# A macaron block on one core: W2 sums in four column groups, the b2 rows by a broadcast load, and the slot table ahead of the expert list

## The chip, the cores and the metric

One of the cores of a Trainium2 chip runs the kernel. The metric is the device time of one execution in microseconds (us); three executions of the kernel before were timed, and their median stands for it.

## The reference, cut to what matters

The input x has 8 batches of 256 tokens of 128 numbers. The whole is a macaron: x + 0.5 FFN(norm x), then x + attention(norm x), then x + 0.5 FFN(norm x), with the same FFN weights in both halves. The FFN is a mixture of 8 experts, of which each token takes the 2 with the largest router logits:

```
logits = xt @ Wr + br;  probs, idx = top_k(softmax(logits), 2)
h = layernorm(relu(xt @ W1[e] + b1[e])) * g1[e] + be1[e]      # 512 wide
y = layernorm(relu(h @ W2[e] + b2[e])) * g2[e] + be2[e]       # 128 wide
out = sum over the token's two experts of gate * y
```

The kernel folds the inner layernorm's g1 and be1 into W2 and b2. The product of a normalized row with g1*W2 needs W2's rows scaled by g1, less their mean over the 512 rows (the sum of g1*W2 over the rows, divided by 512), and b2 needs the sum of be1*W2 added. These sums over the rows of W2, for g1 and for be1 and for each of 8 experts, are the "W2 sums" of this change.

## The kernel before, in words

Each engine runs its own program, in an order written out by hand, and waits on semaphores. The span has a front (routing of all tokens for the first FFN, and preparing the weights), then 39 tiles of 128 sorted token slots in pairs through the experts (first FFN), then attention, then the second FFN. Only the front changes.

The front in the order of the engines:

- SyncE issues the loads: x, Wr, the rows g1, be1, b1 (into `rows`, 96 partitions), b1 again, b2 (one row, into partition 16 of `wmix`), be2, W1 (2 MB), W2 (2 MB), the attention weights, and later the store of the normalized rows.
- GpSimd clears `wmix` (L2410), builds `ones` and the identity, issues the broadcast loads of br and g2, builds the two selection matrices `sel17` and `mask16` and the other constants, splits b1 (`bias_parts`), waits until all 16 tiles are normalized, builds tables and `mask_factors`, adds the last count to `s_ld_a` (L2480), and then gathers the rows of the tiles with indirect transfers (L513), two tiles for each pair.
- TensorE runs 30 products of `ones` (L2495) once the identity is there, then in turns the transposes of the normalized rows (L943) and the logits (L950), the centred W1 of experts 0 to 2 (`hidden_weights`, L2351 and L2352), the ranks, W1 of experts 3 to 5, the first W2 sums (L2378), the 32 slot products (L1037), W1 of experts 6 and 7, the second W2 sums, the transposed gates (L1046), and the first pairs with the "own products" (L1111, L1112) between them.
- The W2 sums are four accumulating products for each half of the experts. Each has 16 columns of `cols` as its stationary operand (g1 and be1 of 8 experts for one chunk of 128 rows) and 4 experts of W2 (512 columns) as its moving one, and they add up in one bank, rows 0 to 15. ScalarE then masks the rows (`own_rows`, L715) into `wmix`. TensorE's own products spread them: with `sel17[0]` to the mean over all partitions (bank 3 or 4), with `sel17[1]` to the be1 sums plus the b2 row of partition 16 (bank 6 or 7).
- VectorE does the layernorm statistics (L1187) and rows (L1196), the choice of the experts, ranks and slot positions, and the one-hot operands of the slot products (L1342 to L1346). After them come the sorted experts (L1348 to L1357), the lambda of attention (L1359, L1360), the slot table (L1362 to L1365), the packed expert numbers (L1216 to L1220), the gates (L1269 to L1276), and the two halves of `center_weights` (L2369), which subtract the spread mean from the scaled W2.
- ScalarE copies between PSUM and SBUF, scales W2 by g1 (L802, 32 tiles of 128x128), then does the exponentials of gates and lambda (L809, L811), `own_rows(0)`, W1 of experts 6 and 7 back, the first copy of turned rows (L747), `own_rows(1)`, and the two copies into `b2p` (L876).

The first pair's transposes of the hidden rows (`turn_h`) wait for the first copy into `b2p`; `hidden(1, ...)` waits for both halves of the centring, and `second(0, ...)` for the second copy.

Of the kernel before, what the change touches and what calls it, by code (L numbers as in the profile page):

```python
# [17 lines left out]
ALU = mybir.AluOpType  # L18
ACT = mybir.ActivationFunctionType
X = mybir.AxisListType.X  # L20
# [88 lines left out]
def build(nc, x, Wq, Wk, Wv, Wo, lq1, lk1, lq2, lk2, Wr, br, W1, b1, g1, be1, W2, b2, g2, be2, out, stages=("f1", "at", "f2")):  # L109
    with ExitStack() as ctx:  # L110
# [26 lines left out]
        cols = sb("cols", [P, 96])  # L137
# [3 lines left out]
        mask16 = sb("mask16", [16, NE])  # L141
# [183 lines left out]
        past8 = ordering[0:1, 1344:1344 + 48]  # L325

# [19 lines left out]
        N_IDENT, N_REP, N_EPS, N_MASK, N_CENTER, N_ROWS, NCONST, N_ORDER = 1, 2, 3, 5, 6, 12, 16, 17  # L346
        NMASK, NBIAS = 18, 10
# [432 lines left out]
        def moe_scalar(act, S, first):  # L780
# [3 lines left out]
            if first:  # L784
                deviations(act, S, 0, 4)
                for g in range(1, 4):
                    deviations(act, S, g, 4)
                    turned_rows(act, S, g - 1, first)
                    if g == 1:
                        act.wait_ge(s_cols, 1)  # L790
                        act.copy(cols[:], bank[6][:, 0:96]).then_inc(s_colc, 1)
# [15 lines left out]
                scaled(1)  # L807
                act.wait_ge(S["top"], 1)
# [5 lines left out]
                own_rows(act, 0)  # L814
# [182 lines left out]
        def moe_tensor(pe, S, first):  # L997
# [3 lines left out]

            if first:
                turn_rows(pe, S, 0, first)
                pe.wait_ge(s_ld_w, 16 * 7)
# [28 lines left out]
                weight_sums(pe, 0, range(FC))  # L1033
# [75 lines left out]
            def own_products(h):  # L1109
                pe.wait_ge(s_mixed, h + 1)  # L1110
                pe.matmul(bank[3 + h][:], sel17[:, 0, :], wmix[:, 512 * h:512 * h + 512], start=True, stop=True).then_inc(s_wmix, 1)  # L1111
                pe.matmul(bank[6 + h][:], sel17[:, 1, :], wmix[:, 512 * h:512 * h + 512], start=True, stop=True).then_inc(s_b2m, 1)  # L1112

            if first:
                pe.wait_ge(s_colc, 2 + NE - 1)
                turn_x(0, 0, 0)
                own_products(0)
# [3 lines left out]
                own_products(1)  # L1121
# [4 lines left out]
                turn_x(2, 1, 0)  # L1126
                pe.wait_ge(s_w2c, 2)
                hidden(1, 1, e[2:4])
# [158 lines left out]
        def first_routing(dve, S, step):  # L1287
# [59 lines left out]

            step.begin(dve.tensor_tensor(ends16[0:1, 0:NE], offsets[0:1, 0:NE], rows16[0:1, 0:NE], ALU.add))  # L1348
# [9 lines left out]
            dve.wait_ge(s_ld_a, 80)  # L1358
            step(dve.tensor_tensor(lam_p[:], lam_in[:, 0:4:2, :], lam_in[:, 1:4:2, :], ALU.mult))  # L1359
            dve.tensor_reduce(lam_s[:], lam_p[:], X, ALU.add).then_inc(A["lam"], 1)  # L1360
            dve.wait_ge(S["slotp"], 1)
            step(dve.tensor_copy(slot_t[:], bank[5][:, 0:40]))  # L1362
            step(dve.scalar_tensor_tensor(slot_f[:], bank[5][:, 40:80], float(YBASE), slot_t[:], ALU.mult, ALU.add))
            step(dve.tensor_scalar(slot_i[:], slot_f[:], float(TOPK * TOK - YBASE), None, ALU.add))
            dve.tensor_scalar(slot_u[:], slot_i[:], TOPK * TOK - 1, 1, ALU.bitwise_and, ALU.logical_shift_right).then_inc(S["slot"], 1)  # L1365
# [965 lines left out]
        def bias_parts(pool, st):  # L2331
            pool.wait_ge(s_dve, 1)
            pool.wait_ge(s_ld_w, 16 * 7)
# [26 lines left out]

        def center_weights(dve, step):
            dve.wait_ge(s_bc, 16)
            w2cv = w2c[:].rearrange("p (a c d) -> p a c d", a=NE, c=FC)
            for h in range(2):
# [6 lines left out]
                last.then_inc(s_w2c, 1)  # L2371

# [159 lines left out]
```

## Time and profile before

| | us |
|---|---|
| three executions | 447.38, 447.42, 450.34 |
| median | 447.42 |
| profiled execution: span from first to last instruction | 444.6 |
| TensorE busy in the span | 395.1 |
| VectorE busy in the span | 348.4 |

The profiled execution has no time of its own on the page; its span is 2.8 us under the median, and these 2.8 us lie before the first and behind the last instruction. The span is cut into 40 slices on the page; TensorE is at 70% or more in all of them, and its granted clock is full but for two stretches, one in the front and one early in attention. In the views that follow times count from the span's start.

### The profile page before, as it was taken

The numbers are of one execution on the slowest core, as the hardware profiler recorded it, in microseconds if no ns is written. First come the engines' busy times: TensorE is split into PE (matmuls) and PEld (weight loads), VectorE is DVE, ScalarE is ACT, GpSimd is POOL, SyncE is SP. The second block draws the span as 40 slices with busy tenths as digits, with TensorE's granted clock in tenths as the row PEclk, the third lists the DMA queues.
The fourth block names the chain that finished last, engine by engine and source line by source line (L and its number), as shares of the span: only waits on it lengthen the run. The fifth ranks groups of instructions, "written<-read, shape, count | busy, mean of one in ns | idle before, by whom it ended". The sixth has DMA issues, their size and how long they took to land.

```text
span 444.6 us, 11683 instructions
## 1 busy us (share of the span) xinstructions
PE 395.1 (89%) x3605; PEld 278.5 (63%) x3606; DVE 348.4 (78%) x1302; ACT 286.7 (64%) x589; POOL 246.8 (56%) x348
## 2 busy tenths in 40 slices
PE   7989999999898857889888889976899899999984
PEld 7735487877676744556564656554577677878733
DVE  5886578887959886878897988976688968788865
ACT  1395687755676754787677777764765467667630
POOL 8685554436461136374847566576634758555540
PEclk9996999999999955999999999999999899999999
DMA  7920114554443411000000001001121221111127
GB/s 219 335 96 14 35 49 143 181 178 158 121 144 112 170 37 35 21 8 20 25 13 25 24 21 33 25 27 36 56 60 34 72 64 56 53 59 47 37 72 244
DMA packets 25862, 35.17 MB, mean 79 GB/s; under 512 B 4282, under 2 KB 18546, under 8 KB 24659
## 3 DMA queue, kind: packets, MB, share of 16 engines
q1 hardware_dynamic: 20866, 24.62, 16.7%
q0 software_dynamic: 4944, 9.90, 7.6%
q8 instruction: 28, 0.46, 0.4%
q14 instruction: 24, 0.19, 0.1%
HBM read 15.45 MB, written 18.24 MB: 76 GB/s over the span
## 4 chain that ended last, share of the span: by engine, by line
PE 51%; DVE 20%; issue 9%; POOL 8%; ACT 5%; DMA 3%; DVEq 1%; SPq 1%; POOLq 0%; ACTq 0%
PE bank L972 11%; PE bank L991 10%; PE bank L981 5%; DVE mx L2134 4%; POOL xr_scratch L459 3%; PE bank L1181 3%; PE bank L2495 2%; PE bank L1900 2%; DMA early<-y_scratch 2%; PE bank L1176 2%; ACT early L1712 1%; PE bank L1918 1%; POOL orr L1658 1%; PE bank L1852 1%; DMA y_scratch<-yo,dest_u 1%
## 5 line engine op out<-in xcount | busy, mean ns | idle before, releaser
L991 PEld LDWEIGHTS bank<-w2c,hT 128*128 128x128 f32 x624 | 76.5, 194 | 23.5 <-issue 22.6
L991 PE MATMUL bank<-w2c,hT 128*128 x624 | 78.1, 279 | 4.9 <-ACT hT L760 4.9
L972 PE MATMUL bank<-w1s,xT 128*128 x156 | 74.1, 596 | 0.7 <-DVE w2c L2369 0.6
L2134 DVE TENSOR_REDUCE mx<-bank 128x4 f32<-128x1024 f32 (+1 forms) x48 | 58.5, 1220 | 13.7 <-PE bank L1861 13.3
L1712 ACT ACTIVATE early<-bank 128x768 f32<-128x768 f32 x64 | 51.8, 812 | 23.7 <-PE bank L1908 23.0
L1377 DVE BATCH_NORM_STATS2 st<-wide 128x6 f32<-128x512 f32 x78 | 50.1, 683 | 19.8 <-ACT wide L754 19.7
L760 ACT COPY hT<-bank 128x1024 f32<-128x1024 f32 (+1 forms) x40 | 39.5, 988 | 34.0 <-PE bank L981 34.0
L513 POOL DMA_INDIRECT xgw<-xn_scratch,slot_u x39 | 37.4, 960 | 35.4 <-PE bank L961 24.3
L483 POOL DMA_INDIRECT y_scratch<-yo,dest_u x39 | 39.0, 1001 | 31.3 <-PE bank L981 16.8
L579 POOL DMA_INDIRECT yk<-y_scratch,posi x32 | 32.2, 1005 | 42.2 <-DMA y_scratch<-yo 17.4
L754 ACT ACTIVATE wide<-bank 128x1024 f32<-128x1024 f32 (+1 forms) x40 | 40.0, 1001 | 10.3 <-PE bank L972 9.6
L459 POOL DMA_INDIRECT xr_scratch<-row_buf,hi_i x32 | 31.8, 994 | 22.6 <-PE bank L1908 12.9
L981 PE MATMUL bank<-ident,wide 128*128 128x128 f32 x312 | 40.9, 274 | 1.3 <-issue 1.3
L972 PEld LDWEIGHTS bank<-w1s,xT 128*128 128x128 f32 x156 | 27.0, 190 | 22.0 <-issue 21.6
L981 PEld LDWEIGHTS bank<-ident,wide 128*128 128x128 f32 x312 | 35.3, 142 | 2.6 <-issue 2.0
L937 ACT COPY wide<-bank 128x1024 bf16<-128x1024 bf16 x28 | 28.4, 1014 | 5.7 <-PE bank L1181 5.6
L775 ACT ACTIVATE yo<-yz,r 128x128 f32<-128x128 f32 x78 | 27.1, 396 | 4.2 <-DVE yz L1420 2.6
L1396 DVE SCALAR_TENSOR_TENSOR yy<-bank,r,b2p 128x128 f32<-128x128 f32 x78 | 24.6, 351 | 6.1 <-DVE r L1390 1.6
L1900 PE MATMUL bank<-mxT,sel 64*128 64x384 bf16 x128 | 22.2, 343 | 7.2 <-ACT early L1712 5.1
L1852 PE MATMUL bank<-mrhs,mlhs 64*128 64x128 bf16 (+1 forms) x192 | 16.1, 248 | 11.4 <-DVE mx L2134 6.6
L1420 DVE SCALAR_TENSOR_TENSOR yz<-yy,mv,g2b 128x128 f32<-128x128 f32 x78 | 23.3, 339 | 0.0
L559 POOL TENSOR_TENSOR ars<-ave,neg_half 128x2 f32<-128x2 f32 x8 | 5.8, 720 | 31.2 <-DVE ave L2092 31.2
(380 smaller groups left out, 893.4 us busy)
## 6 DMA issues: line engine op xcount, KB each, us to landing
xr_scratch<-row_buf SPq DMA_DIRECT2D x8, 1032.0 KB
xgw<-xr_scratch SPq DMA_DIRECT2D x39, 64.5 KB, 1.8
y_scratch<-yo SPq DMA_DIRECT2D x19, 128.0 KB, 1.8
w1s<-in_L_ffn_W_dram SPq DMA_DIRECT2D x1, 2048.0 KB, 9.9
early<-y_scratch SPq DMA_DIRECT2D x8, 256.0 KB, 3.4
xn_scratch<-row_buf SPq DMA_DIRECT2D x1, 1024.0 KB
out_dram<-xs SPq DMA_DIRECT2D x8, 128.0 KB, 2.6
row_buf<-row_buf SPq DMA_DIRECT2D x6, 128.0 KB
```

Of the source, the lines that this page charges most:

```text
L459: pool.indirect_dma_start(out=xr_dram, out_offset=bass.IndirectOffsetOnAxis(ap=slot2[:, c:c + 1], axis=0), in_=rows_of[t // HALF][:, t % H ...
L483: pool.indirect_dma_start(out=y_dram, out_offset=bass.IndirectOffsetOnAxis(ap=dest_u[:, 2 * p + j:2 * p + j + 1], axis=0), in_=yo[:, p % 2 ...
L513: pool.indirect_dma_start(out=xg[:, u, :], out_offset=None, in_=xn_dram, in_offset=bass.IndirectOffsetOnAxis(ap=slot_u[:, n:n + 1], axis=0 ...
L579: pool.indirect_dma_start(out=yk4[:, t % (2 * YRING), k, :], out_offset=None, in_=done, in_offset=bass.IndirectOffsetOnAxis(ap=posi[:, c:c ...
L754: act.activation(hh[:, u, 0:k, :], banks[:, h_at[u]:h_at[u] + k, :], ACT.Relu).then_inc(S["relu"], 1)
L760: act.copy(hT[:, u, 0:k, :], banks[:, 5:5 + k, :]).then_inc(S["hTc"], 1)
L972: last = pe.matmul(bank[h_at[u] + j][:], xT[:, u, j, :], w1s[:, bass.ds(e * FF, FF)], start=True, stop=True)
L981: last = pe.transpose(bank[5 + j][:, c * P:c * P + P], hh[:, u, j, c * P:(c + 1) * P], ident[:])
L991: last = pe.matmul(o[:, j * DIM:(j + 1) * DIM], hT[:, u, j, c * P:(c + 1) * P], w2c[:, bass.ds(e * (FC * DIM) + c * DIM, DIM)], start=(c = ...
L1377: last = dve.bn_stats(st1[:, u, j, :], hh[:, u, j, :])
L1712: act.activation(prob[:, g], quad[:, low:low + 2, 0:3 * P], ACT.Exp).then_inc(A["prob"], 1)
L2134: dve.tensor_reduce(mx[:, c:c + 2 * per].rearrange("p (a q) -> p q a", q=2), quad[:, low:low + 2, :].rearrange("p q (a e) -> p q a e", a=p ...
```

## The change

1. The W2 sums no longer add up in one group of 16 rows. Each of the four products of a half takes its own group of 32 columns of the TensorE array (`tile_position=(0, 32 * c)`) and writes its own 32 rows of the bank. The 32 columns are those of g1, be1 and b1 and of a fourth, zero block. Each half has a bank of its own (6 and 2), and both halves come before the slot products.
2. The adding up over the four chunks moves into the own products: `wmix` now has 128 rows, `mask16` and `sel17` repeat in each group of 32 rows, and VectorE builds them (`row_masks`, 9 instructions) from the identity before x lands. GpSimd's clearing of `wmix` and its 5 instructions for the masks are gone.
3. b2 no longer goes through `wmix`. GpSimd issues one broadcast load of b2 into `b2p` behind `bias_parts`, SyncE's load of the row goes, and VectorE adds the be1 sums to `b2p` after the centring (two additions of 128x512); ScalarE's two copies go.
4. Both `own_rows` come right behind the scaling of W2 on ScalarE, and both own products right behind W1 of experts 6 and 7 on TensorE, instead of around the first pair. `hidden(1, ...)` no longer waits for the centring; `second(0, ...)` does.
5. On VectorE the lambda and the slot table come before the sorted experts instead of behind them.

```diff
@@ constants
-        cols = sb("cols", [P, 96])
-        mask16 = sb("mask16", [16, NE])
+        mask16 = sb("mask16", [P, NE])
+        bands = ordering[:, 1400:1400 + 4 * NE].rearrange("p (c e) -> p c e", c=4)
+        band_sums = ordering[:, 1440:1440 + 6]
+        cols = ordering[:, 1536:1536 + P]
@@ own_rows (ScalarE)
-                last = act.activation(wmix[0:16, e * DIM:(e + 1) * DIM], bank[6 + h][0:16, a * DIM:(a + 1) * DIM], ACT.Copy,
+                last = act.activation(wmix[:, e * DIM:(e + 1) * DIM], sums_bank(h)[:, a * DIM:(a + 1) * DIM], ACT.Copy,
                                       scale=mask16[:, e:e + 1])
@@ moe_scalar
                 scaled(1)
+                act.wait_ge(s_dve, ROW_MASKS)
+                own_rows(act, 0)
+                own_rows(act, 1)
                 act.wait_ge(S["top"], 1)
...
                 act.wait_ge(s_const, NCONST)
-                own_rows(act, 0)
                 hidden_weights_back(act, range(6, 8))
...
                 copy_xT(0, 0)
-                own_rows(act, 1)
-
-                def own_b2(h):
-                    act.wait_ge(s_b2m, h + 1)
-                    act.copy(b2p[:, 512 * h:512 * h + 512], bank[6 + h][:]).then_inc(s_mixed, 1)
-
-                own_b2(0)
                 relu(0, 0)
-                own_b2(1)
                 copy_xT(1, 1)
@@ moe_tensor
                 hidden_weights(pe, range(3, 6))
-                weight_sums(pe, 0, range(FC))
+                weight_sums(pe, 0)
+                weight_sums(pe, 1)
                 for c in range(TOPK * TT):
...
                 hidden_weights(pe, range(6, 8))
+                pe.wait_ge(s_dve, ROW_MASKS)
+                own_products(0)
                 pe.wait_ge(s_colc, 2 + 6)
-                weight_sums(pe, 1, range(FC))
+                own_products(1)
...
                 turn_x(0, 0, 0)
-                own_products(0)
...
                 hidden(0, 0, e[0:2])
-                own_products(1)
                 turn_x(1, 0, 1)
...
                 turn_x(2, 1, 0)
+                hidden(1, 1, e[2:4])
                 pe.wait_ge(s_w2c, 2)
-                hidden(1, 1, e[2:4])
                 pe.wait_ge(s_mixed, 4)
                 second(0, 0, e[0:2])
@@ first_routing (VectorE): these eight lines move from behind the sorted experts to before them
+            dve.wait_ge(s_ld_a, 80)
+            step(dve.tensor_tensor(lam_p[:], lam_in[:, 0:4:2, :], lam_in[:, 1:4:2, :], ALU.mult))
+            dve.tensor_reduce(lam_s[:], lam_p[:], X, ALU.add).then_inc(A["lam"], 1)
+            dve.wait_ge(S["slotp"], 1)
+            step(dve.tensor_copy(slot_t[:], bank[5][:, 0:40]))
...
@@ new functions, and the end of center_weights
+        def row_masks(dve, step):
+            dve.wait_ge(s_const, N_IDENT)
+            quarter = ident[:].rearrange("p (c i) -> p c i", c=4)
+            g_rows, be_rows = band_sums[:, 4:5], band_sums[:, 5:6]
+            step.begin(dve.memset(cols[:, 96:P], 0.0))
+            step(dve.tensor_tensor(bands, quarter[:, :, 0:NE], quarter[:, :, NE:2 * NE], ALU.add))
+            step.begin(dve.tensor_reduce(mask16[:], bands.rearrange("p c e -> p e c"), X, ALU.add))
+            step(dve.tensor_reduce(band_sums[:, 0:4], quarter[:, :, 0:NE], X, ALU.add))
+            step.begin(dve.tensor_reduce(g_rows, band_sums[:, 0:4], X, ALU.add))
+            step(dve.tensor_reduce(be_rows, mask16[:], X, ALU.add))
+            step(dve.tensor_tensor(be_rows, be_rows, g_rows, ALU.subtract))
+            step.begin(dve.tensor_scalar(sel17[:, 0, :], ones[:], g_rows, 1.0 / FF, ALU.mult, ALU.mult))
+            step.begin(dve.tensor_scalar(sel17[:, 1, :], ones[:], be_rows, None, ALU.mult))
...
-            dve.wait_ge(s_bc, 16)
+            dve.wait_ge(s_bc, 32)
...
+            for h in range(2):
+                dve.wait_ge(s_b2m, h + 1)
+                own = b2p[:, 512 * h:512 * h + 512]
+                dve.tensor_tensor(own, own, bank[6 + h][:], ALU.add).then_inc(s_mixed, 1)
+        def sums_bank(h):
+            return bank[(6, 2)[h]]
-            for c in chunks:
-                last = pe.matmul(bank[6 + h][0:16, :].rearrange("p (a d) -> p a d", d=DIM), cols[:, c:c + 61:4], w2s[:, 4 * h:4 * h + 4, c, :],
-                                 start=(c == 0), stop=(c == FC - 1))
+            for c in range(FC):
+                last = pe.matmul(sums_bank(h)[32 * c:32 * c + 32, :].rearrange("p (a d) -> p a d", d=DIM), cols[:, c:c + 125:4],
+                                 w2s[:, 4 * h:4 * h + 4, c, :], start=True, stop=True, tile_position=(0, 32 * c))
@@ SyncE
-            sp.wait_ge(s_const, N_IDENT)
-            sp.dma_start(wmix[16:17, :], b2.rearrange("(o a) d -> o (a d)", o=1)).then_inc(s_ld_w, 16)
@@ GpSimd
-            st(pool.memset(wmix, 0.0))
...
-            st(pool.affine_select(out=sel17[:, 0, :], in_=ones[:], compare_op=ALU.is_ge, fill=0.0, base=NE - 1,
-                                  pattern=[[0, P]], channel_multiplier=-1))
...
             bias_parts(pool, st)
+            pool.dma_start(b2p[:], b2.rearrange("(o a) d -> o (a d)", o=1).to_broadcast([P, NE * DIM])).then_inc(s_bc, 16)
@@ VectorE, start
             step(dve.memset(row_buf[1][:, 0:NE * FF // 2], 0.0))
+            row_masks(dve, step)
```

## Rows read from the trace of the kernel before

**Rows 1.** Windows, start:end, us; busy (count) of PE, PEld, DVE, ACT, POOL; clock, DMA, GB/s.

```profile
62.00:110.00 48.00, 48.00 (x296) 36.28 (x295) 39.20 (x173) 32.80 (x71) 21.72 (x23) 1.00 0.44 149
```

**Rows 2.** Chain that ended last, within 0 to 62 us: start, us, what.

```profile
41.89 3.55 PE bank L2378 x8
...
47.64 1.72 PE bank L972 x4
...
55.05 1.78 PE bank L991 x16
56.83 0.87 PE bank L981 x8
```

**Rows 3.** Timeline 0 to 30 us: start, us, engine, line, operation, [idle before it].

```profile
0.81 0.95 POOL L2410 MEMSET early<- 128x1024 f32 x1 [0.29 <-POOLq L2522]
...
3.50 0.58 POOL L2418 DMA_DIRECT2D g2b<-in_L_ffn_g_dram  x1
...
7.28 0.87 DVE L1187 BATCH_NORM_STATS2 stats<-xs 128x6 f32<-128x128 f32 x4 [4.21 <-DMA xs<-in_L_attn_x_dram]
...
17.22 0.23 DVE L1300 TENSOR_TENSOR lg<-bank,brb 128x64 f32<-128x64 f32 x1 [0.64 <-PE bank L950]
```

**Rows 4.** DMA view by queue: 5 to 6 us, then 6 to 7 us.

```profile
q1 hardware_dynamic: 184, 0.28, 107.2%
...
q0 software_dynamic: 85, 0.25, 79.9%
```

**Rows 5.** Timeline 24.5 to 62 us, TensorE around the sums and slot products.

```profile
28.29 3.62 PE L2378 MATMUL bank<-early,cols 128*16 128x512 f32 x8
...
32.39 5.20 PE L1037 MATMUL bank<-turned_o,wide 128*128 128x80 bf16 x32 [0.48 <-DVE turned_o L1346]
```

**Rows 6.** Timeline of TensorE, 260.6 to 262.1 us: column-tiled products in attention.

```profile
260.65 0.64 PE L1918 MATMUL bank<-early,vaug 128*32 128x256 f32 x8
261.10 0.61 PE L1920 MATMUL bank<-early,vaug 128*32 128x256 f32 x8
```

**Rows 7.** Windows, columns as in Rows 1.

```profile
31.47:34.88 3.41, 2.93 (x18) 2.25 (x16) 3.27 (x7) 3.39 (x12) 3.04 (x5) 1.00 0.00 0
...
38.29:41.70 3.41, 3.41 (x6) 0.98 (x4) 3.00 (x17) 3.04 (x8) 1.18 (x2) 0.50 0.01 2
...
170.00:180.00 10.00, 9.66 (x95) 5.45 (x94) 5.15 (x13) 5.22 (x10) 6.54 (x10) 0.59 0.10 27
```

**Rows 8.** Timeline 24.5 to 62 us, VectorE's chain and GpSimd's last count.

```profile
34.87 0.15 DVE L1348 TENSOR_TENSOR yk<-yk 1x8 f32<-1x8 f32 x1
...
37.06 0.09 POOL L2480 MEMSET pads<- 1x1 f32 x1
...
38.21 0.18 DVE L1359 TENSOR_TENSOR lam_p<-lam_in 128x16 f32<-128x16 f32 x1
...
38.51 0.19 DVE L1362 COPY slot_t<-bank 128x40 f32<-128x40 f32 x1
...
39.28 0.17 DVE L1216 TENSOR_SCALAR eidf<-eidf 1x48 f32<-1x48 f32 x1
...
41.79 0.15 DVE L1209 TENSOR_SCALAR neg_lam<-neg_lam 128x1 f32<-128x1 f32 x1
...
46.98 2.48 DVE L2369 TENSOR_TENSOR w2c<-w2c,bank 128x512 f32<-128x512 f32 x4 [5.04 <-PE bank L1111]
```

**Rows 9.** The same timeline, ScalarE.

```profile
34.69 1.28 ACT L809 ACT_TABLE_LOAD   x1
...
40.25 1.09 ACT L715 ACTIVATE early<-bank,mask 16x128 f32<-16x128 f32 x4
...
45.95 0.38 ACT L747 ACTIVATE xT<-bank 128x256 f32<-128x256 f32 x1
...
49.39 1.02 ACT L754 ACTIVATE wide<-bank 128x1024 f32<-128x1024 f32 x1 [1.13 <-PE bank L972]
```

**Rows 10.** DMA issues, 0 to 70 us: count, median us from issue to landing.

```profile
xgw<-xn_scratch,slot_u POOLq DMA_INDIRECT x16, 2.6
```

More of the change, by code:

```diff
@@ L344, in build @@
         block = ctx.enter_context(nc.Block())
-        N_IDENT, N_REP, N_EPS, N_MASK, N_CENTER, N_ROWS, NCONST, N_ORDER = 1, 2, 3, 5, 6, 12, 16, 17
-        NMASK, NBIAS = 18, 10
+        N_IDENT, N_REP, N_EPS, N_CENTER, N_ROWS, NCONST, N_ORDER = 1, 2, 3, 4, 10, 14, 15
+        NMASK, NBIAS, ROW_MASKS = 18, 10, 10
         ROWS = 16 * 2 * TOPK
@@ L790, in moe_scalar @@
                         act.wait_ge(s_cols, 1)
-                        act.copy(cols[:], bank[6][:, 0:96]).then_inc(s_colc, 1)
+                        act.copy(cols[:, 0:96], bank[6][:, 0:96]).then_inc(s_colc, 1)
                         act.wait_ge(s_cols, 2)
@@ L1000, in keep_warm, with own_products @@
                     pe.matmul(bank[bk][:], ones16[:], iota_rep[:, 0:64, :].rearrange("p a b -> p (a b)"), start=True, stop=True)
+            def own_products(h):
+                pe.wait_ge(s_mixed, h + 1)
+                pe.matmul(bank[3 + h][:], sel17[:, 0, :], wmix[:, 512 * h:512 * h + 512], start=True, stop=True).then_inc(s_wmix, 1)
+                pe.matmul(bank[6 + h][:], sel17[:, 1, :], wmix[:, 512 * h:512 * h + 512], start=True, stop=True).then_inc(s_b2m, 1)
             if first:
                 turn_rows(pe, S, 0, first)
-                pe.wait_ge(s_ld_w, 16 * 7)
+                pe.wait_ge(s_ld_w, 16 * 6)
                 pe.wait_ge(s_const, N_REP)
@@ L1107, in shared_bias @@
                 pe.matmul(at, gsT[:], be2x[:, 4 * q:4 * q + 4, :], start=True, stop=True).then_inc(S["be2"], 1)
[L1109 to L1112, printed above, removed]
             if first:
@@ L1346, in first_routing @@
                 dve.tensor_scalar(oh_hi[:, 1, :, c], oh_hi[:, 1, :, c], row_id[:], None, ALU.mult).then_inc(S["oh"], 1)
+            dve.wait_ge(s_ld_a, 80)
[3 more added lines that the diff above has]
+            step(dve.tensor_copy(slot_t[:], bank[5][:, 0:40]))
+            step(dve.scalar_tensor_tensor(slot_f[:], bank[5][:, 40:80], float(YBASE), slot_t[:], ALU.mult, ALU.add))
+            step(dve.tensor_scalar(slot_i[:], slot_f[:], float(TOPK * TOK - YBASE), None, ALU.add))
+            dve.tensor_scalar(slot_u[:], slot_i[:], TOPK * TOK - 1, 1, ALU.bitwise_and, ALU.logical_shift_right).then_inc(S["slot"], 1)
             step.begin(dve.tensor_tensor(ends16[0:1, 0:NE], offsets[0:1, 0:NE], rows16[0:1, 0:NE], ALU.add))
@@ L1357, in first_routing @@
             step(dve.tensor_tensor(eidf[:], eidf[:], past8, ALU.subtract))
[L1358 to L1365, printed above, removed]
             pack_experts(dve, S, step, 0, 40)
@@ L2359, in build @@
         W1_BANKS = (0, 1, 7)
+        def row_masks(dve, step):
[11 more added lines that the diff above has]
+            step.begin(dve.tensor_scalar(sel17[:, 1, :], ones[:], be_rows, None, ALU.mult))
+            assert step.n == ROW_MASKS, step.n
         def center_weights(dve, step):
-            dve.wait_ge(s_bc, 16)
+            dve.wait_ge(s_bc, 32)
             w2cv = w2c[:].rearrange("p (a c d) -> p a c d", a=NE, c=FC)
@@ L2371, in center_weights, with weight_sums @@
                 last.then_inc(s_w2c, 1)
-        def weight_sums(pe, h, chunks):
+            for h in range(2):
[4 more added lines that the diff above has]
+            return bank[(6, 2)[h]]
+        def weight_sums(pe, h):
             pe.wait_ge(s_colc, 2)
             pe.wait_ge(s_ld_w2, 16)
-            for c in chunks:
-                last = pe.matmul(bank[6 + h][0:16, :].rearrange("p (a d) -> p a d", d=DIM), cols[:, c:c + 61:4], w2s[:, 4 * h:4 * h + 4, c, :],
-                                 start=(c == 0), stop=(c == FC - 1))
-            if c == FC - 1:
-                last.then_inc(s_wmix, 1)
+            for c in range(FC):
+                last = pe.matmul(sums_bank(h)[32 * c:32 * c + 32, :].rearrange("p (a d) -> p a d", d=DIM), cols[:, c:c + 125:4],
+                                 w2s[:, 4 * h:4 * h + 4, c, :], start=True, stop=True, tile_position=(0, 32 * c))
+            last.then_inc(s_wmix, 1)
         b1s = early[0:32, 5760:5760 + P]
```

8 lines of the change are left out of this document (1 added, 7 removed).

## Prediction

> **What bounds the kernel now.** I read the windows first. From 62 to 110 us TensorE is busy in 48.00 of 48.00 us [rows 1], so whatever the front gives or takes reaches the expert loop in full. Then the chain of waits: up to 62 us it runs through the warm-up products, the logits, VectorE's routing, the slot products, W1 of experts 6 and 7, the second W2 sums (41.89 to 45.44) and the first pair, whose `second(0)` starts at 55.05 us [rows 2]. That start is my yardstick: what it moves by, the end moves by. Last the timeline, for what waits just beside the chain: VectorE sits idle for 5.04 us before the centring [rows 8], and the first sums (28.29 to 31.91) lie in time that TensorE would spend waiting for the one-hots anyway, since the slot products start at 32.39 when VectorE is ready [rows 5].
>
> **The W2 sums.** A half is 8 records, 3.55 us on the chain [rows 2, 5]. The trace of before has the new form in attention: 8 records of 128x256 in groups of 32 columns, and the next 8 start 0.45 us later [rows 6]; in turn they would take half of 3.55, 1.78 us. For 512 columns that is 2 x 0.45 = 0.9 us a half, 1.8 us for both: 28.3 to 30.1. All of it is hidden before 32.39. Bounds for both halves: 1.8 us, and in turn 7.1 us, to 35.4. I take 1.8, since those rows are of the same kind and size of group.
>
> The Trainium skill, "TensorEngine Tiling (Array Packing)", "Key Properties", says that a change of tiling mode drains the engine. No separate price for it can be read here, and with 2.3 us of slack in front of the slot products it would not enter the sum.
>
> **TensorE behind the slot products.** Their start and end (32.39 and 37.59) stay: the second 16 wait for one-hots ready at about 35. W1 of experts 6 and 7 stays, to 41.89 [rows 2, 5]. In place of the second sums (3.55) come four own products. A product of 128x512 is half of 1.72, 0.86 us [rows 2], so 3.45 us: TensorE is at 45.35, as before. The gain is behind that: the four products are gone from around the first pair. The gates and the first x turned take about 0.5 (45.85), ScalarE's copy 0.38 [rows 9], now uncovered (46.3), `hidden(0)` 1.72 (48.0), relu 1.02 and a start (49.1) [rows 2, 9]. Before, relu started at 49.39 and the turn of h came at about 51.1.
>
> **VectorE becomes the one that decides.** Its one-hots end at 34.9. The lambda comes next and waits for GpSimd's count, 37.06 + 0.09 [rows 8]. Queued behind that wait is all of VectorE's work, but the slot products end only at 37.59, so it costs 2.2 us of useful time for the sorted experts and nothing for the slot table. Then, all from rows 8:
> - lambda 38.51 - 38.21 = 0.3, done at 37.5; the slot table then waits for 37.6 and takes 39.28 - 38.51 = 0.8: 38.4 (before 39.3);
> - sorted experts 38.21 - 34.87 = 3.35, now behind it: 41.75;
> - packed experts, gates, neg_lam 41.94 - 39.28 = 2.65: 44.4. The gates are ready about 44.2, before TensorE wants them at 45.35;
> - the centring needs the first mean at 41.89 + 0.86 = 42.75, which is there: 44.4 + 2 x 2.48 = 49.4 (before 52.7);
> - two additions of 128x512. No such addition of b2 is in the trace; the centring's own 128x512 instructions take 2.48 / 4 = 0.62 each, so 50.0 and 50.65. Bounds 0.5 to 0.8 each.
>
> The turn of h waits for the first addition, 50.05, not for relu at 49.1. Then 0.87 for it [rows 2], 0.2 for the next x, 1.72 for `hidden(1)`: `second(0)` starts at 52.9. The copy of hT (ready about 51.9), the centring (49.4) and the second addition (50.65) are earlier. Gain 55.05 - 52.9 = 2.15 us.
>
> **Edits at nothing, and their cover.** `row_masks`: 9 small VectorE instructions of 0.1 to 0.3 us, 2 us at most, in the 4.21 us of idle before x [rows 3]. Both `own_rows`: 1.09 us each [rows 9], on ScalarE behind the scaled W2 (34.7), to 36.9; the exponentials move 2.2 us back to about 38.5, wanted by VectorE at 42.7, and W1's copies back end with the products at about 42.5, wanted at 46.3. The slot table 0.9 us sooner lets the gathers of the second pair be issued by about 44.2 and land 2.6 us later [rows 10], 46.8, before the 48.0 at which they are turned; no gain in itself. The broadcast of b2 (0.5 MB) goes out behind `bias_parts`, beside the loads of W1 and W2; at the 0.25 to 0.28 MB a microsecond of [rows 4] it is some 2 us of transfer, and W2 could land that much later: 0 to 2 us on ScalarE's scaling, whose `own_rows` then end by 38.9, wanted at 41.9. Cover enough, with 3 us left.
>
> **The start.** Without the clearing of `wmix` the identity comes 0.95 us sooner [rows 3], and so do the warm-up products. VectorE waits 0.64 us for the logits at 17.22 [rows 3], which is all that this can give: 0.6. Against it, the load of g2 is issued 0.95 us sooner too. x's queue moved 0.28 MB in the microsecond from 5 to 6, and g2's took 79.9% of the engines in the next one [rows 4]; overlapped, x could land up to 0.9 us later. VectorE would then end its rows at 17.5 in place of 16.6, a loss of 0.3. Bounds -0.6 and +0.4; I take 0, as x later by about half of that leaves the start of the choice near 17.1.
>
> **The sum.** Against the profiled execution's span: 444.6 - 2.15 + 0 = 442.4. With the 2.8 us around the span, and from the median of 447.42, this is **445.2 us**.
>
> **TensorE's clock** was full to 34.88, half until 41.70, and full again after the busy products of W1 [rows 7]. The slot products take 2.6 us for 16 at either level, and only W1 of experts 6 and 7 pays. Now TensorE idles from 30.1 to 32.4 before the light slot products. Should the clock fall sooner, nothing there takes longer, and the same W1 products come before its return. The Trainium skill, "TensorE: Matmul & The Clock Gate", Part 1, warns of gaps between bursts, after which the engine runs at half rate; by it this change could only bring the fall forward, and the sum by that is the same.
>
> **Rivals.**
> - *Only TensorE counts.* GpSimd's last table instructions run beside an idle VectorE and its chain is quicker than its rows say, so the turn of h follows relu at 49.1: gain 3.1, with up to 0.6 of the start 443.7 to 444.3. For it: only 0.9 us separate the two. Against: every length in the chain is a row's.
> - *The column groups run in turn* (the slower side). The sums then end at 35.4 and the slot products (32 in 5.2 us [rows 5]) at 40.6 in place of 37.6; the slot table, sorted experts, gates and centring all follow, 3.0 us later. 3.0 - 2.15 = 0.85 us slower: 448.3. It decides from the point at which both sums take more than about 6.2 us. Against it: rows 6.
> - *The clock in attention.* In 170 to 180 us TensorE is busy for 9.66 us at a mean clock of 0.59 [rows 7], so it returns there at about 178. If the return falls differently against the work that now comes 2 us sooner, one such stretch (as in rows 7, 3.4 us) more or less at half costs or gives at most half of it, 1.7 us: 443.5 or 446.9. One of the three executions of before was 2.9 us above the others, so something of this size exists; I can't tell whether it is this.
> - *It doesn't arrive.* The change does what it says, but a wait I hold to be covered (gates, W2 under the added b2 load, x under g2) is the last, and eats 1.5 to 2.2 us: 446.7 to 447.5. The gates have 1.2 us of slack, the others' is not read from a row.
>
> **How the numbers follow.** Forecast (444.5 to 446.2) 0.45; only TensorE 0.13; groups in turn 0.07; clock 0.18, half to each side; not arriving 0.12; the rest 0.05. The range takes in all named cases: 443.0 to 448.3. About 1% (4.5 us) is what a measurement of this kernel can tell from no change. No named case reaches it on either side; summed favourably, 3.1 + 0.6 + 1.7 gives 5.4 us, so I hold faster by over 1% at 0.07, slower at 0.03, within at 0.90.
>
> **What would show each step.** Both sums (8 + 8 records) within about 2 us from 28.3, slot products still at 32.4 to 37.6; slot table by 38.5 and the first gather near 39.4; VectorE without a gap from 37.6 to 50.7; the turn of h released by the addition into `b2p`; `second(0)` at about 52.9; x's wait on VectorE ending between 7.3 and 8.2. Wrong would be: the sums reaching past 32.4, the centring released by TensorE, not by VectorE's own work, or a `second(0)` at 52.9 with an end that has not moved, which would put the cause behind the front.

## The result, and the profile after

| | before | after |
|---|---|---|
| median of 15 executions each, us | 448.26 | 446.03 |
| lowest to highest, us | 445.91 to 450.38 | 443.95 to 449.98 |
| ratio, 95% interval | | 0.9954 [0.9932, 0.9975] |
| span of the profiled execution, us | 444.6 | 447.0 |
| its mean granted clock of TensorE | 0.965 | 0.958 |

By the ratio the change makes the kernel 2.06 us faster (1.1 to 3.0), which is under 1%; the medians differ by 2.23. The ratios here and below leave disturbed executions out (at most two of a series, but four of 12 in "The second half later") and are not quotients of the two medians shown. The execution that was profiled after the change is the longest of its 15, so its span can't be set against that of before; what can be compared is the order of the steps and their times in the front.

The chain that ended last, of the changed kernel, 0 to 62 us (start, us, what):

```profile
37.31 0.10 POOL pads L2489
...
37.44 0.19 DVE lam_p L1346
...
37.82 0.12 DVE slot_t L1349
...
38.60 0.06 DVE yk L1353
...
41.76 0.19 DVE eidf L1213
...
44.53 0.15 DVE w2c L2382
44.69 0.45 issue
45.14 4.22 DVE w2c L2382 x7
49.36 0.66 DVE b2p L2388
50.01 0.09 issue
50.10 1.17 PE bank L977 x8
51.27 0.43 PE bank L957 x2
51.70 3.09 PE bank L968 x4
54.79 1.78 PE bank L987 x16
```

Read it beside [rows 2] and [rows 8]. The chain now lies on VectorE from 37.44 to 50.01, with one piece of 0.45 us put down to issue, and goes over to TensorE at the turn of h. The last line is `second(0)`: 54.79 against 55.05, only 0.26 us sooner.

The timeline of the changed kernel around this (start, us, engine, line, operation, [idle before it <- what ended it]):

```profile
6.89 0.87 DVE L1184 BATCH_NORM_STATS2 stats<-xs 128x6 f32<-128x128 f32 x4 [2.22 <-DMA xs<-in_L_attn_x_dram]
...
22.90 0.29 DVE L1311 TENSOR_TENSOR picked<-oh 128x128 bf16<-128x128 f32 x1
...
27.72 1.95 PE L2398 MATMUL bank<-early,yk 128*32 128x512 f32 x16
...
31.79 2.61 PE L1039 MATMUL bank<-turned_o,wide 128*128 128x80 bf16 x16 [2.11 <-DVE turned_o L1343]
...
34.60 2.58 PE L1039 MATMUL bank<-turned_o,wide 128*128 128x80 bf16 x16 [0.21 <-DVE turned_o L1343]
...
44.98 0.38 ACT L749 ACTIVATE xT<-bank 128x256 f32<-128x256 f32 x1
...
45.71 1.98 PE L968 MATMUL bank<-w1s,xT 128*128 x4 [0.77 <-ACT xT L749]
...
50.10 1.17 PE L977 MATMUL bank<-ident,wide 128*128 128x128 f32 x8 [2.20 <-DVE b2p L2388]
51.31 1.01 ACT L762 COPY hT<-bank 128x1024 f32<-128x1024 f32 x1 [1.13 <-PE bank L977]
51.49 3.30 PE L968 MATMUL bank<-w1s,xT 128*128 x4
```

All 16 records of both sums take 1.95 us, where 8 of the old form took 3.62 [rows 5]; TensorE then waits 2.11 us for the one-hots, so the sums are hidden. In front of the turn of h it waits again, 2.20 us, for the addition into `b2p`. Right behind that wait four products of W1 take 3.09 us on the chain; elsewhere they take 1.72 [rows 2].

Windows of the changed kernel (columns as in rows 1; the one before the last is the DMA share):

```profile
49.00:50.00 1.00, 0.00 (x0) 0.00 (x0) 1.00 (x3) 1.00 (x5) 0.70 (x2) 1.00 0.13 41
50.00:51.00 1.00, 0.90 (x8) 0.93 (x9) 1.00 (x3) 0.18 (x1) 1.00 (x2) 0.96 0.09 25
51.00:52.00 1.00, 1.00 (x5) 0.83 (x4) 0.96 (x5) 0.69 (x1) 1.00 (x1) 0.50 0.24 66
52.00:53.00 1.00, 1.00 (x2) 0.34 (x1) 0.09 (x2) 0.61 (x2) 0.78 (x4) 0.50 0.00 0
53.00:54.00 1.00, 1.00 (x2) 0.34 (x1) 0.00 (x0) 0.00 (x0) 0.69 (x2) 0.50 0.00 0
54.00:55.00 1.00, 1.00 (x6) 0.71 (x5) 0.00 (x0) 0.17 (x1) 0.89 (x1) 0.83 0.24 66
...
62.00:110.00 48.00, 48.00 (x297) 36.36 (x296) 38.79 (x172) 32.92 (x72) 22.04 (x24) 1.00 0.45 153
```

TensorE's granted clock was full while it idled, stood at 0.50 (1.2 of 2.4 GHz) from 51 to 54 us, though TensorE was busy there in every microsecond, and came back between 54 and 55. The expert loop is as before: busy in 48.00 of 48.00 us [rows 1].

### The profile page after: what moved, and what is told of

Same layout as the page of the kernel before. It is cut to its first block, busy times and chain, and to the rows that moved or that the text cites. A ratio compares the mean times of both kernels' runs of the same rounds, so it can differ in the third digit from the quotient of the medians.

```text
span 447.0 us, 11684 instructions
## 1 busy us (share of the span) xinstructions
PE 393.5 (88%) x3601; PEld 279.8 (63%) x3606; DVE 350.7 (78%) x1313; ACT 285.7 (64%) x587; POOL 246.4 (55%) x343
## 4 chain that ended last, share of the span: by engine, by line
PE 55%; DVE 15%; ACT 5%; issue 5%; POOL 5%; DMA 3%; DVEq 1%; SPq 0%; POOLq 0%; ACTq 0%
PE bank L968 13%; PE bank L987 13%; PE bank L977 7%; DVE mx L2131 4%; PE bank L1178 3%; PE bank L1897 2%; PE bank L1173 2%; ACT early L1709 2%; DMA early<-y_scratch 2%; PE bank L957 2%; PE bank L1915 2%; PE bank L1849 1%; PE bank L1917 1%; POOL orr L1655 1%; PE bank L1919 1%
## 5 line engine op out<-in xcount | busy, mean ns | idle before, releaser
L968 PE MATMUL bank<-w1s,xT 128*128 x156 | 75.6, 606 | 0.8 <-ACT xT L749 0.8
L515 POOL DMA_INDIRECT xgw<-xn_scratch,slot_u x39 | 37.9, 973 | 34.3 <-PE bank L957 24.5
L461 POOL DMA_INDIRECT xr_scratch<-row_buf,hi_i x32 | 31.8, 995 | 24.5 <-PE bank L1905 14.6
```

The costliest lines, as they stand in the source:

```text
L461: pool.indirect_dma_start(out=xr_dram, out_offset=bass.IndirectOffsetOnAxis(ap=slot2[:, c:c + 1], axis=0), in_=rows_of[t // HALF][:, t % H ...
L515: pool.indirect_dma_start(out=xg[:, u, :], out_offset=None, in_=xn_dram, in_offset=bass.IndirectOffsetOnAxis(ap=slot_u[:, n:n + 1], axis=0 ...
L968: last = pe.matmul(bank[h_at[u] + j][:], xT[:, u, j, :], w1s[:, bass.ds(e * FF, FF)], start=True, stop=True)
```

## Experiments

The theory after this reading: the steps of the prediction hold, VectorE decides the turn of h, and TensorE's wait there costs a fall of the clock in some executions. Rivals: the gain has to do with the sums alone, the start gives all of it, or the order of the slot table is what pays. Edits are shown against the changed kernel, unless said otherwise.

**Sorted experts first.** The order of VectorE goes back to that of before (part 5 of the change undone).

```diff
@@ first_routing: the eight lines return to where they were
-            dve.wait_ge(s_ld_a, 80)
-            step(dve.tensor_tensor(lam_p[:], ...
...
             step(dve.tensor_tensor(eidf[:], eidf[:], past8, ALU.subtract))
+            dve.wait_ge(s_ld_a, 80)
+            step(dve.tensor_tensor(lam_p[:], ...
...
             pack_experts(dve, S, step, 0, 40)
```

> The changed kernel with one part undone: on VectorE the sorted experts come before the lambda and the slot table again, as in the kernel before. Theory (VectorE's chain decides): the sorted experts, 3.2 us, run again while VectorE waits for the slot products, the centring starts when the first mean is there (about 41.9) and not at 44.5, the second addition ends near 48.2 in place of 50.6, and the turn of h follows relu at 48.8 in place of 50.1. That is 1.3 us, and TensorE's wait before it shrinks from 2.2 to 0.9 us, so that the clock falls less often there: 443.9 to 444.8, a ratio to before of 0.990 to 0.992. Rival (the slot table decides, by the gathers): the first gather starts 0.8 us later, and the time is 0.8 us above that of the changed kernel, a ratio near 0.997. Rival (neither): ratio 0.995 as the changed kernel.

Measured: 443.75 us, ratio to before 0.9917 [0.9887, 0.9946]. Timeline of this kernel:

```profile
42.57 4.87 DVE L2382 TENSOR_TENSOR w2c<-w2c,bank 128x512 f32<-128x512 f32 x8 [0.52 <-PE bank L1000]
47.36 1.28 DVE L2388 TENSOR_TENSOR b2p<-b2p,bank 128x512 f32<-128x512 f32 x2
48.05 1.02 ACT L756 ACTIVATE wide<-bank 128x1024 f32<-128x1024 f32 x1 [2.36 <-PE bank L968]
...
49.22 1.06 PE L977 MATMUL bank<-ident,wide 128*128 128x128 f32 x8 [0.99 <-ACT wide L756]
```

The sorted experts lie again in VectorE's wait for the slot products. The centring starts 1.96 us sooner (44.53 to 42.57), until it is itself released by TensorE's first mean, and the turn of h is released by relu, which ended at 49.08: the moment that the prediction gave to its rival "only TensorE counts". TensorE's wait is 0.99 us, the clock stays full (1.00 in 45 to 56 us), and `second(0)` starts at 52.22. So part 5 costs time, and VectorE was the decider.

**The sums four times.** The 16 products are issued four times over, 64 in all (each bank is written again with the same values).

```diff
-            for c in range(FC):
+            for c in 4 * list(range(FC)):
```

> The changed kernel with the products of the W2 sums issued four times over (the same values each time), so that they take as long as they would with the column groups in turn. Theory: 64 records at some 0.11 us are 7.2 us, from 27.7 to 34.9; the slot products start 3.1 us later and end near 40.1; VectorE's slot table, sorted experts, gates, centring and additions follow, and second(0) starts 2.5 to 3 us later: 3 us above the changed kernel, 448.5 to 449, a ratio to before of 1.000 to 1.003. Against that TensorE is never idle in front of the slot products, so its clock may stay full through W1 of experts 6 and 7, which gives nothing, since VectorE is last. Rival (the sums have cover enough, or W1 at full clock makes up for it): ratio 0.995, as the changed kernel.

Measured: 448.11 us, 1.0011 [0.9987, 1.0036]. Timeline of this kernel:

```profile
27.96 7.10 PE L2398 MATMUL bank<-early,yk 128*32 128x512 f32 x64
...
35.00 4.95 PE L1039 MATMUL bank<-turned_o,wide 128*128 128x80 bf16 x32
...
39.98 0.20 DVE L1349 COPY slot_t<-bank 128x40 f32<-128x40 f32 x1 [1.97 <-PE bank L1039]
...
52.35 1.06 PE L977 MATMUL bank<-ident,wide 128*128 128x128 f32 x8 [1.84 <-DVE b2p L2388]
```

This puts the sums at 7.1 us, the length of the rival "the groups run in turn". The slot table comes 2.24 us later than in the changed kernel, and `second(0)` starts at 55.36 with a clock that stays full behind a wait of 1.84 us. That is 0.3 us behind before; the rival was priced at 0.85. So the sums are free only as long as they end ahead of the one-hots, and with slow sums the whole gain of the change is gone, whatever its other parts do. No run took parts 3 and 4 (b2's way and the moved waits) out singly; their shares are read from the traces only.

**The wait filled.** Nine products of a constant go in front of the wait for the addition (they write a bank that is not in use).

```diff
                 pe.wait_ge(S["gTc"], 1)
+                keep_warm(9, 5)
                 pe.wait_ge(s_mixed, 3)
```

> The changed kernel with 9 products of 128x512 (bf16, of constants) on TensorE in the 2.2 us in which it waits for the addition into b2p. Theory (TensorE's idle stretch there lets its clock fall, in some executions, for the turn of h and hidden(1)): the profiled clock stays full from 45 to 56 us, second(0) starts at about 52.7 in place of 54.6, and the median falls by 0.5 to 1.5 us: ratio 0.992 to 0.994. Rival (the fall comes from elsewhere or costs nothing on the median): ratio 0.995, and a fall in the clock near 51 is seen all the same. If the products last longer than the wait the turn of h starts later than the addition allows, at most 0.2 us.

Measured: 446.92 us, 0.9961 [0.9934, 0.9988]. In the chain of this kernel:

```profile
48.60 1.94 PE bank L996 x9
50.54 0.87 PE bank L977 x8
51.63 1.72 PE bank L968 x4
53.35 1.78 PE bank L987 x16
```

The wait is gone, the clock stays full, the four W1 products take 1.72 us again, `second(0)` is at 53.35. The time is nevertheless that of the changed kernel (0.9954, 0.9959 and 0.9956 in its three series). So the fall explains the late `second(0)` of the profiled execution after the change, 1.69 us of the 3.95 by which that execution is above its median; no effect on the median shows, though the interval here, 0.27% to either side (1.2 us), could hide a small one.

**b2 between the halves.** The first addition comes between the two halves of the centring.

```diff
                 last.then_inc(s_w2c, 1)
-            for h in range(2):
+                dve.wait_ge(s_wmix, 4)
                 dve.wait_ge(s_b2m, h + 1)
```

> The changed kernel with the first addition into b2p moved between the two halves of the centring (the second stays behind them). Theory (the turn of h waits for that addition, which is queued behind 4.9 us of centring): it ends at 47.6, the turn of h follows relu at 48.8 in place of 50.1, second(0) starts 1.2 us sooner, when the centring (50.0) and the second addition (50.65) are ready: 444.0 to 444.9, ratio to before 0.990 to 0.993. Rival (the centring's own end decides, for second(0)): ratio 0.995 as the changed kernel, with TensorE waiting before second(0) and not before the turn of h.

Measured: 444.63 us, 0.9922 [0.9894, 0.9949]. Timeline of this kernel:

```profile
44.84 2.48 DVE L2382 TENSOR_TENSOR w2c<-w2c,bank 128x512 f32<-128x512 f32 x4
47.24 0.68 DVE L2388 TENSOR_TENSOR b2p<-b2p,bank 128x512 f32<-128x512 f32 x1
47.84 2.48 DVE L2382 TENSOR_TENSOR w2c<-w2c,bank 128x512 f32<-128x512 f32 x4
...
49.24 1.06 PE L977 MATMUL bank<-ident,wide 128*128 128x128 f32 x8 [0.99 <-ACT wide L756]
```

The order of the slot table is that of the changed kernel here, and the turn of h still comes at 49.24, released by relu; `second(0)` at 52.24. (The added wait on `s_wmix` holds the first addition back until both means are there.) Two edits with nothing in common but VectorE's path to the first addition give the same start and the same time.

**The clearing put back.**

```diff
             st = Steps(pool, s_pool)
+            st(pool.memset(wmix, 0.0))
```

> The changed kernel with GpSimd's clearing of wmix (0.95 us, nothing needs it now) put back ahead of the identity. Theory (the sooner identity is a part of the gain, through the warm-up products and the logits): the warm-up ends near 11.7 in place of 10.8, VectorE's picked experts come 0.5 us later than in the changed kernel (22.9), second(0) and the end as much: 446.5, ratio to before 0.996 to 0.997. Rival (the start gives nothing on the median, since x lands at a time of its own and the load of g2 takes back what the identity gives): ratio 0.995 as the changed kernel. A difference of 0.5 us is near what five rounds can tell; the profile's times of picked and of x's landing are the better witness.

Measured: 447.51 us, 0.9972 [0.9938, 1.0006]. The choice of the experts (`picked`) starts at 23.48 us, as before (23.46), against 22.90 in the changed kernel. From there the whole front is later by the same amount: the lambda starts at 37.99 for 37.44, the turn of h at 50.66 for 50.10. The interval of the ratio takes in both theories and no change at all, so only the profile speaks for the first. The chain of this kernel shows the same fall behind the wait as the changed one:

```profile
50.66 1.68 PE bank L977 x8
52.34 0.43 PE bank L957 x2
52.77 2.57 PE bank L968 x4
55.34 1.78 PE bank L987 x16
```

**Before, with the slot table first.** The kernel before with part 5 of the change alone.

```diff
@@ before.py, first_routing: the eight lines move ahead of the sorted experts
+            dve.wait_ge(s_ld_a, 80)
...
             step.begin(dve.tensor_tensor(ends16[0:1, 0:NE], ...
```

> The kernel before with the fifth part of the change alone: lambda and slot table ahead of the sorted experts on VectorE. Theory (TensorE decides there, with its second sums and own products): the slot table is 0.9 us sooner, the gates are ready near 44.2, TensorE wants them at 45.4; the centring starts at 47.0 with the first mean as before. Nothing moves: ratio 0.998 to 1.002, second(0) at 55.0. Rival (the sooner slot table is worth something by itself, by the gathers): ratio 0.998 or less. Rival (it costs, as it does in the changed kernel): ratio 1.003 or more, with VectorE and not TensorE releasing the centring.

Measured: 447.67 us, 0.9987 [0.9963, 1.0012]; `second(0)` at 55.15. In the kernel before VectorE had 5.04 us to spare ahead of the first half of the centring [rows 8], and there the order costs nothing and gives nothing. The second half was on the path in the kernel before as well, behind TensorE's second own products, and this line of its timeline, which the prediction doesn't use, shows what part 4 takes away:

```profile
53.07 1.98 PE L972 MATMUL bank<-w1s,xT 128*128 x4 [0.59 <-DVE w2c L2369]
```

**Both edits.** Sorted experts first and b2 between the halves.

> The changed kernel with both edits that were faster by themselves: sorted experts ahead of the slot table again, and the first addition into b2p between the halves of the centring. Theory: either alone already brings the turn of h to relu (49.2 in both profiles), so the second gives nothing more: ratio 0.991 to 0.993, second(0) at 52.2. Rival (they add up, by VectorE being free sooner for the statistics of the first pair): ratio 0.988 to 0.990.

Measured: 445.48 us, 0.994 [0.9911, 0.9969]; turn of h at 49.48 behind 0.99 us of wait for relu, `second(0)` at 52.49. In the trace they don't add, as each alone already brings relu to the front. The ratio is above the 0.991 to 0.993 of the theory: the mean of its 12 executions (445.60, standard error 0.45) lies 1.1 to 1.3 us above those of the single edits (below), about twice the error of such a difference (0.6); neither the front nor the expert loop shows why.

**The second half later.** Sorted experts first, the second own products behind the first `hidden`, b2 between.

```diff
                 own_products(0)
-                pe.wait_ge(s_colc, 2 + 6)
-                own_products(1)
...
                 hidden(0, 0, e[0:2])
+                own_products(1)
                 turn_x(1, 0, 1)
@@ center_weights: b2 between, with another wait ahead of it
-            for h in range(2):
+                dve.wait_ge(s_colc, 2 + 7)
                 dve.wait_ge(s_b2m, h + 1)
```

> The same two edits, and the second own products (1.7 us) moved back behind hidden(0), where TensorE otherwise waits 1.0 us for relu. Theory (with VectorE out of the way TensorE's own order decides, up to the landing of the first gather): the first x is turned near 44.3, when its second gather lands, in place of 44.9; hidden(0) ends near 46.6, the second products fill TensorE's wait for relu, the turn of h starts near 48.4 and second(0) at 51.4, if the centring's second half (from 47.5 to 50) and addition (50.7) are ready: 0.8 us under the version with both edits, ratio 0.989 to 0.991. Rival (VectorE decides again, since the second mean comes later): second(0) waits for the centring or the addition and starts at 51.8 or later, no gain: ratio 0.992.

Measured: 445.79 us median of 12, 0.9913 [0.9879, 0.9946] from eight of them, so the ratio says little. Timeline of this kernel:

```profile
45.70 1.98 PE L968 MATMUL bank<-w1s,xT 128*128 x4 [0.99 <-ACT xT L749]
...
49.45 1.04 PE L977 MATMUL bank<-ident,wide 128*128 128x128 f32 x8
```

`hidden(0)` starts at 45.70, 0.6 us sooner than with both edits (46.30) and not 1.7: TensorE now waits for the gather of the first x, which landed at 44.34. From there to the end of `hidden(0)` (47.68) it takes 3.3 us, where the theory allowed 2.3, as it left out most of the turning and the handoffs. The moved products then take 1.72 us, longer than the wait for relu that they fill (0.99), and the turn of h starts at 49.45, against 49.48 with both edits. `second(0)` is at 52.57, not at the 51.4 that the theory expected: the gather is the next bound of `hidden(0)`, and the moved products that of the turn of h.

**Repeats**, on another chip, of the changed kernel (twice), of sorted first and of b2 between.

> The changed kernel as it is, once more, for its profile and to stand on one chip beside the two edits. Theory: turn of h released by VectorE's first addition at 50 to 50.4 after a wait of 2.2 us; where the clock falls just then, second(0) starts near 54.8 to 55.3, where it does not, near 53.1; ratio to before 0.994 to 0.997.

> The version with the sorted experts ahead of the slot table once more. Theory: the turn of h follows relu at 49.2, second(0) at 52.2 to 52.5, 0.7 us sooner than the changed kernel at full clock and 2.5 us sooner than the changed kernel whose clock fell: ratio to before 0.990 to 0.994, under the changed kernel of the same call by 1 to 2 us. Rival (its first ratio of 0.992 was luck): ratio 0.995, no different from the changed kernel.

> The version with the first addition between the halves of the centring once more. Theory: as the version with the sorted experts first, ratio 0.990 to 0.994. Rival: 0.995, no different from the changed kernel.

> The changed kernel a second time in this call, for a third profile: how often the clock falls during TensorE's wait before the turn of h, and how far two series of one kernel lie apart. Theory: ratio 0.994 to 0.997, within 0.002 of the other series of it.

Measured: changed kernel 446.39 us, 0.9959 [0.993, 0.9988] and 446.38 us, 0.9956 [0.9931, 0.9982]; sorted first 445.19 us, 0.9921 [0.9893, 0.9949]; b2 between 443.81 us, 0.9924 [0.9894, 0.9954]. The two edits hold: in this series too they are 0.0032 to 0.0038 under the changed kernel, some 1.4 to 1.7 us. Two of the four profiles missed the times expected for them. In the first repeat of the changed kernel and in sorted first again TensorE's clock was at half for some 3 us already ahead of the sums (about 21 to 25 us, and 20 to 23 us), and the slot products started only at 33.96 and 33.63; in sorted first again it was then at half until 44 us, too, through W1 of experts 6 and 7. So their `second(0)` come late, at 56.43 and 54.51. The last series, the changed kernel again, has a profile without a fall behind the wait. Its timeline, and below it the one of the first repeat of the same program:

```profile
50.55 1.06 PE L977 MATMUL bank<-ident,wide 128*128 128x128 f32 x8 [2.13 <-DVE b2p L2388]
```

```profile
51.74 1.58 PE L977 MATMUL bank<-ident,wide 128*128 128x128 f32 x8 [2.15 <-DVE b2p L2388]
```

Nearly the same wait (2.13 and 2.15 us), and from the turn of h to `second(0)` 3.00 us in the one and 4.69 in the other.

**The profiles side by side.** The first transposes of attention come at about 110 us. The distance from `second(0)` to them, and what is left from them to the end of the span:

| profile | turn of h waits, us | second(0) | transposes | distance | to the end |
|---|---|---|---|---|---|
| before | | 55.05 | 111.92 | 56.87 | 332.7 |
| before, slot table first | | 55.15 | 111.95 | 56.80 | 332.8 |
| changed | 2.20 | 54.79 | 111.56 | 56.77 | 335.4 |
| changed, first repeat | 2.15 | 56.43 | 113.24 | 56.81 | 336.6 |
| changed, second repeat | 2.13 | 53.55 | 110.32 | 56.77 | 334.3 |
| clearing put back | 2.14 | 55.34 | 112.10 | 56.76 | 336.4 |
| wait filled | none | 53.35 | 110.11 | 56.76 | 336.3 |
| sums four times | 1.84 | 55.36 | 112.13 | 56.77 | 336.0 |
| sorted first | 0.99 | 52.22 | 109.08 | 56.86 | 331.0 |
| sorted first, again | 0.99 | 54.51 | 111.37 | 56.86 | 331.7 |
| b2 between | 0.99 | 52.24 | 109.06 | 56.82 | 333.1 |
| b2 between, again | 0.99 | 52.62 | 109.44 | 56.82 | 332.1 |
| both | 0.99 | 52.49 | 109.25 | 56.76 | 332.5 |
| the second half later | none | 52.57 | 109.34 | 56.77 | 335.4 |

The distance is 56.76 to 56.87 us in all of them. What the start of `second(0)` moves by, all of the expert loop moves by. What is left behind it is not constant: 331.0 to 336.6 us, a spread wider than any difference in the fronts. In the six profiles with the longest rest (335.4 and more) the granted clock fell once more between 100 and 140 us behind the transposes; in the other eight it was full there. Whether an edit in the front changes how often that happens, these single profiles can't tell.

## Why the prediction was right, and where it was not

**The forecast and its size.** 445.2 us was forecast from a median of 447.42, a gain of 2.15 us. Measured were 446.03 us beside a median of 448.26 for before in the same series, a gain of 2.23 us by the medians and 2.06 by the ratio. The absolute forecast is 0.8 us low, which is the 0.84 by which the three executions at the start lay under the 15 of the series. The time is inside the range, and "within 1%" came true. That the size came so close is in part luck: the interval runs from 1.1 to 3.0 us, and the forecast was a gain in `second(0)`, which no profile of the changed kernel has in full. With the clock full and the start about as late as before (second repeat, `picked` at 23.38) it is 55.05 - 53.55 = 1.50 us.

**The steps.** Both sums: 1.8 us forecast, 1.95 measured, ended at 29.7 and hidden. Sorted experts done at 41.75 forecast, 41.76 measured; gates and the rest 44.4, 44.51; centring 49.4, 49.36; first addition 50.0, 50.01 at 0.66 us; turn of h 50.05, 50.10, released by the addition into `b2p`. So VectorE decided, by the path that was worked out for it. From there to `second(0)` 2.85 us were forecast; it is 3.00 at a full clock (second repeat).

**Two terms were mis-sized and cancel.** For the start I took 0, between -0.6 and +0.4. x did not land later under the earlier load of g2: VectorE's wait for it ended at 6.89 us in the changed kernel and between 6.97 and 7.43 in the others with that load, against 7.13 with the clearing put back and 7.28 before [rows 3], so it was mostly outside the 7.3 to 8.2 that I had named as the sign. `picked` starts at 22.90 to 23.25 us in eight profiles with the earlier identity and at 23.36 to 23.52 in three more; with the later one it starts at 23.41 to 23.48 in three. That is 0.3 us on average, and 0.56 in the profiled execution. The second term is GpSimd's count. The lambda's wait for it, which I had held to end before the slot products, became the last by 0.2 us: the memset was at 37.31 in place of 37.06 [rows 8], although everything had begun 0.56 us sooner, and with the start of before (clearing put back) it was at 37.87, 0.8 us late. Why GpSimd gets there later is open. In the profiled execution the two misses, 0.6 us for and 0.8 against, leave 0.2, which the sorted experts gave back (3.16 us in place of 3.35). The agreement of the later steps to 0.1 us is therefore luck; with the clearing put back the same steps come at 42.30, 49.95 and 50.66.

**TensorE's new wait was not followed up.** The prediction had TensorE finish `hidden(0)` at 48.0 and the turn of h at 50.05, so the wait of 2 us was in its own numbers. I priced the clock in front of the slot products and in attention, and not there. In three of the four profiles with this wait the clock fell behind it (changed, first repeat, clearing put back), at a price of 1.69 us: 54.79 - 50.10, 56.43 - 51.74 and 55.34 - 50.66 are 4.68 to 4.69 us, against 3.00. It never fell behind a wait of 0.99 us (five profiles), nor where the wait was filled, nor behind 1.84 us. The Trainium skill, "TensorE: Matmul & The Clock Gate", Part 1, says that waits between bursts of products bring the engine back to half rate; three of these four profiles agree, and the fourth, with a wait of 2.13 us, shows that the same wait does not do it each time. How often it falls in executions that nobody profiled is open: the three with the fall took 449.98, 452.2 and 450.28 us, 2.8 to 5.8 us above their medians, the one without it 446.34, but 1.69 us of that is all that this fall can explain; and the filled wait made no gain in 12 executions.

**Part 5 was held to be free ("no gain in itself"), and it costs about 2 us.** This is where the reasoning stopped short, though the price was in the sum: I wrote that the lambda's wait cost "2.2 us of useful time for the sorted experts" and left it at that. Undone, `second(0)` starts at 52.22 us, and with b2 between at 52.24 and 52.62, which is 0.9 to 1.3 us sooner than in the changed kernel at a full clock (53.55). The mean of 11 executions is 444.34 us (standard error 0.44) against 446.36 (0.28) for 38 of the changed kernel: 2.0 us, with an error of 0.5. With the execution of 449.77 us, which is not among the 11, it would be 1.6. b2 between the halves: 444.51 (0.39) in 13. What exceeds the 0.9 to 1.3 us of the front is within the errors, or comes from the clock, behind the wait or in attention; no run separates these. The slot table 0.9 us sooner bought nothing, as foreseen. In the kernel before the same order cost nothing.

**The handoff of the first x.** ScalarE's copy of 0.38 us was counted, but not the 0.35 us between its end (45.36) and the first product (45.71). It lay beside VectorE's chain and cost nothing in the changed kernel; in the faster versions it is on the path.

**The rivals.** "Only TensorE counts" is refuted for the changed kernel and is what the two faster versions reach: relu ends at 49.08 and 49.10 in the first profile of each, where 49.1 was worked out. "The groups run in turn" is refuted by 1.95 us for 16 records; its price was of the right kind, 0.3 us behind before where 0.85 was expected. Whether the clock in attention moves with the change can't be told: the mean granted clock of the 15 executions after is 0.965, the same as in the profile of before. The one profile of the changed kernel that is near its median reaches attention 1.6 us sooner than that of before, and both have a span of 444.6 us. Behind the transposes it takes 1.6 us longer, and other profiles differ by more there. So single spans can't carry a difference of 2 us; the series can.

## What to carry to other kernels

Before an order on an engine is changed, look at whose idle time the moved work used: the sorted experts cost nothing inside the wait for the slot products and lay on the chain with 3.2 us outside of it. When a sum of one engine's times shows that another will now wait where it did not, follow that wait too, for what lies behind it (here the clock). And let a table of one start against one later mark, over many profiles, say how far a gain in the front carries: here to the end of the expert loop, behind which the profiles differ by more than the gain. Medians that differ by under 0.5% need a dozen executions each; 12 gave a standard error of 0.45 us here.

## What the runs showed of the hardware

- Products of fp32, 128x512, in four groups of 32 columns: 16 records in 1.95 us and 64 in 7.10, 0.11 us each; in one group 8 records took 3.62 [rows 5], 0.45 each. That is four times the rate, and no cost is to be seen where the groups begin: the product before them starts at 27.41 and takes 0.38 us, the first of them starts at 27.72.
- The granted clock can fall to half behind a wait of about 2.15 us although TensorE was busy before and after it: in three of four profiles of the same wait. Behind 0.99 us it stayed full in all five.
- Executions of one program differ by 6 us, and in the main the time goes with the mean granted clock: of the 15 after the change 443.95 us at 0.969, 444.06 at 0.973, 448.03 at 0.957, 449.98 at 0.958. The three profiles of the changed kernel have spans of 444.6 to 449.8 us; of these 5.2 us, 2.9 lie ahead of `second(0)` and 2.3 behind the expert loop.
